# Adding the causal mask of the plain scores on VectorE instead of TensorE in an audio tower's three causal attentions

## The chip, the cores and the metric

The kernel runs on one core of one Trainium2 chip. The metric is the device time of one execution in microseconds (us); the time quoted for a kernel is the median of its runs.

## What is computed

A whole audio encoder: a tokenizer turns 32 utterances of 375 frames into 93 tokens of 256 features, and four layers follow, each an attention-like part and a feed-forward part. What matters here are the four softmax attentions. Three of them are causal, and the mask stands in the reference like this:

```
# layer 0 (16 heads of 16)
scores = jnp.einsum('bhqd,bhkd->bhqk', q, k) * scale
scores = jnp.where(causal[None, None], scores, -jnp.inf)
probs = jax.nn.softmax(scores / TEMP, axis=-1)
# layer 1 (16 heads of 16)
att = jnp.where(causal, att, jnp.float32(-jnp.inf))
att = jax.nn.softmax(att, axis=-1)
# layer 2 (32 maps of 8, taken from each other in pairs)
att = jnp.where(causal, att, -jnp.inf)
att = jax.nn.softmax(att, axis=-1)
```

The attention in the last feed-forward part (16 heads) has no mask. In the kernel's names they are `gattn` (layer 0, gated), `rattn` (layer 1), `dattn` (layer 2, differential) and `eattn` (the one without a mask).

## The kernel before

The layers run one after another on all 32 utterances, with barriers between them. All four attentions share one set of functions, one per engine, and one class `Attention` with their tiles and semaphores. An utterance has 93 tokens; its maps (16, or 32 in `dattn`) are worked on in units of 4, so that one PSUM bank holds 4 x 93 = 372 columns. A unit pair takes the two banks of `ps_s` (plain scores, query on the partitions) and later the two of `ps_t` (transposed scores, key on the partitions). An utterance has 2 pairs in `gattn`, `rattn` and `eattn`, and 4 in `dattn`.

The plain scores serve only for the row maximum. `maximum` (L677) on VectorE (DVE) reduces each bank to 4 negated maxima per row; `split` writes them as two bf16 parts, TensorE (PE) turns them (`turn_max`, L551), `max_t` (L692) copies them out, and the products with `sel` (L570) add them to the transposed scores. ScalarE (ACT) takes the exponential (L657), and the products of `weigh` (L584) make outputs and denominators: 17 columns wide, with a weight load of 93 columns each.

The mask of the plain scores is a product. Before the 8 score products of a pair, PE multiplies a bf16 identity by `mask_q` (0 or -1e30), 372 columns, into each bank (L536), and the scores (L542) add to it. The transposed scores get their mask in `gattn` and `rattn` through `sel` and `maxT` ("merged"), in `dattn` through products with `mask_k` (L559); this stays.

Each engine's order is written out by hand as a software pipeline. In its step for utterance b, PE makes the scores of utterance b+1 pair by pair and the transposed scores and weighted sums of b. Ahead of the last pair's transposed scores it turns the context of utterance b-1 (`turn_ctx`, L595), behind them comes the output projection of b-1 (`project`, L607), and `turn_max` of b+1 ends the step. DVE takes, for each pair, the two maxima of b+1 and then one piece of `behind`, the work on the context of b-1. In `gattn`, `rattn` and `eattn` that is one piece after the first pair: reciprocal and product (L919 and L920 in `gattn`). In `dattn` there are three: `context` after pair 0 (L1484 to L1488), `difference` after pair 1 (L1492 to L1495), then GpSimd (POOL) takes an inverse root (L1420), and `finish` after pair 2 makes the context (L1502). `turn_ctx` waits for it (`ctx_ready`). PE may write the next pair's scores when the maxima of the last pair are taken (`maxed`).

Of the kernel before, what the change touches and what calls it, by code (L numbers as in the profile page):

```python
# [24 lines left out]
ALU = mybir.AluOpType  # L25
AX = mybir.AxisListType

P = 128
# [3 lines left out]
T = 93  # L32
# [4 lines left out]
GT = GU * T  # L37
# [5 lines left out]
class Chain:  # L43


    def __init__(self, eng, sem, base=0):
        self.eng, self.sem, self.base = eng, sem, base
# [249 lines left out]
def measure_dve(dve, shared, b, added, count):  # L297

    dve.wait_ge(added, count)
    dve.bn_stats(shared["stat"][0:T, b, :], shared["hidden"][0:T, b, :])  # L300
# [48 lines left out]
class Attention:  # L349
# [11 lines left out]
    def __init__(self, s, maps, causal, exp_scale):  # L361
        self.maps, self.causal, self.exp_scale = maps, causal, exp_scale
        self.width = D // maps
        self.variants = P // 2 // self.width
        self.units = maps // 4
        self.banks_o = maps // HEADS
        self.q_all = s.sb("q_all", [P, DC, B * T])
        self.k_all = s.sb("k_all", [P, DC, B * T])
        self.v = s.sb("v", [P, B, HEADS, HD + 1])
        self.q = s.sb("q", [P, 2, DC, self.variants, T])  # L370
        self.k = s.sb("k", [P, 2, DC, T])
        self.only = s.sb("only", [P, self.variants])
        self.sel = s.sb("sel", [P, maps, T], BF16)
        self.negmax = s.sb("negmax", [P, maps])

        self.split_width = 2 * maps if maps == HEADS else 2 * maps + 2
        self.split = s.sb("split", [P, self.split_width], BF16)


        self.merged = causal and 2 * maps + T <= P  # L380
        self.maxT = s.sb("maxT", [P, T], BF16)
        self.probs = s.sb("probs", [P, 4, GT])
        self.rden = s.sb("rden", [P, self.banks_o, HEADS])
        self.ctx = s.sb("ctx", [P, 2, D])
        self.ctxT = s.sb("ctxT", [P, DC, T])
        if causal:
            self.mask_q = s.sb("mask_q", [P, 4, T], BF16)
            if not self.merged:
                self.mask_k = s.sb("mask_k", [P, 4, T], BF16)
        self.ps_s = s.ps("scores", [P, 2, 512])  # L390
        self.ps_t = s.ps("scoresT", [P, 2, 512])
        self.ps_o = s.ps("outputs", [P, 2, 512])
        self.ps_g = s.ps("general", [P, 2, 512])
        self.const_ready = s.sem("att_const")
        self.q_done = s.sem("q_done")
        self.k_done = s.sem("k_done")
        self.v_done = s.sem("v_done")
        self.q_ready = s.sem("q_ready")
        self.k_ready = s.sem("k_ready")
        self.v_ready = s.sem("v_ready")  # L400
        self.v_gated = None
        self.ranks_ready = None
        self.cut_ready = s.sem("cut_ready")
        self.scored = s.sem("scored")
        self.maxed = s.sem("maxed")
        self.split_ready = s.sem("split_ready")
        self.max_turned = s.sem("max_turned")
        self.maxT_ready = s.sem("maxT_ready")
        self.scoredT = s.sem("scoredT")
        self.probs_ready = s.sem("probs_ready")  # L410
        self.weighed = s.sem("weighed")
        self.outputs_read = s.sem("outputs_read")
        self.ctx_ready = s.sem("ctx_ready")
        self.ctx_turned = s.sem("ctx_turned")
        self.ctxT_ready = s.sem("ctxT_ready")
        self.out_done = s.sem("out_done")
        self.added = s.sem("added")
        self.biased = s.sem("biased")
        self.half_split = s.sem("half_split")
        self.step = s.sem("att_step")  # L420
# [13 lines left out]
def over_utterances(eng, body):  # L434


    body(0, 0, True, False)
    with eng.Fori(0, B // 2 - 1) as i:
        for j in range(2):
            body(2 * i + j + 1, 1 - j, False, False)  # L440
    body(B - 1, 1, False, True)
# [34 lines left out]
def attention_constants_dve(dve, a, ident):  # L476

    rows = ident[:, :].rearrange("p (h v e) -> p v h e", h=2, v=a.variants)
    dve.tensor_reduce(a.only[:, :], rows, AX.XY, ALU.add).then_inc(a.step, 1)
    dve.sem_inc(a.maxed, 2)  # L480
    dve.sem_inc(a.probs_ready, 2)
    dve.sem_inc(a.weighed, 4)
    dve.sem_inc(a.scoredT, 2 * a.units)
    dve.sem_inc(a.outputs_read, 3 - a.banks_o)
# [42 lines left out]
def attention_pe(pe, a, ident, ident16, w_out, before_out=None, extra_out=None):  # L527


    def scores(b, buf, p):  # L530
        if 2 * p % (a.units // DC) == 0:
            pe.wait_ge(a.cut_ready, DC * b + (2 * p * DC // a.units + 1))
        pe.wait_ge(a.maxed, b * a.units + (2 * p + 2))
        if a.causal:
            for half in range(2):
                pe.matmul(a.ps_s[0:T, half, 0:GT], ident16[:, 0:T], a.mask_q[:, :, :], start=True, stop=False,  # L536
                          skip_group_check=True)
        for j in range(4):
            for half in range(2):
                c, _, v = a.place(2 * p + half)  # L540
                rows = slice(half * P // 2, (half + 1) * P // 2)
                mm = pe.matmul(a.ps_s[0:T, half, j * T:(j + 1) * T], a.q[rows, buf, c, v + j, :], a.k[rows, buf, c, :],  # L542
                               start=not a.causal, stop=True, skip_group_check=True)
                if j == 3:
                    mm.then_inc(a.scored, 1)

# [85 lines left out]
    for p in range(a.units // 2):  # L632
        scores(0, 0, p)
# [36 lines left out]
def attention_dve(dve, a, steps, contexts, add, finish=None, shared=None):  # L670

    def maximum(b, w):
        dve.wait_ge(a.scored, b * a.units + (w + 1))
        dve.tensor_reduce(a.negmax[0:T, a.first_map(w):a.first_map(w) + 4],  # L677
                          a.ps_s[0:T, w % 2, 0:GT].rearrange("p (j t) -> p j t", j=4), AX.X, ALU.max,
                          negate=True).then_inc(a.maxed, 1)

    def split(b):
        dve.wait_ge(a.maxed, 2 + (b + 1) * a.units)
        dve.tensor_copy(a.split[0:T, 0:a.maps], a.negmax[0:T, :]).then_inc(a.half_split, 1)
        dve.wait_ge(a.half_split, b + 1)
        dve.tensor_tensor(a.split[0:T, a.maps:2 * a.maps], a.negmax[0:T, :], a.split[0:T, 0:a.maps],
                          ALU.subtract).then_inc(a.split_ready, 1)
        dve.wait_ge(a.split_ready, b + 1)

    def max_t(b):
        dve.wait_ge(a.max_turned, b + 1)  # L690
        dve.wait_ge(a.scoredT, a.units * (b + 2))
        dve.tensor_copy(a.maxT[0:2 * a.maps, :], a.ps_g[0:2 * a.maps, 0, :].bitcast(BF16)[:, 0:T]).then_inc(a.maxT_ready, 1)  # L692

    def behind(b, buf, p):

        if p == 0:
            dve.wait_ge(a.weighed, 4 + a.units * (b + 1))
            steps.begin(b)
        if p < len(contexts):
            contexts[p](b, buf)  # L700
        if p == len(contexts) - 1:
            steps.end()
        if p == len(contexts) and finish is not None:
            finish(b, buf)

    def utterance(b, buf, first, last):
        for p in range(a.units // 2):
            if not last:
                maximum(b + 1, 2 * p)
                maximum(b + 1, 2 * p + 1)  # L710
            if not first:
                behind(b - 1, 1 - buf, p)
        if not last:
            split(b + 1)
        if not first:
            add(b - 1)
        if not last:
            max_t(b + 1)
        if not first and shared is not None:
            measure_dve(dve, shared, b - 1, a.added, b)  # L720

    for w in range(a.units):
        maximum(0, w)
    split(0)
    max_t(0)
    over_utterances(dve, utterance)
    for p in range(a.units // 2):
        behind(B - 1, 1, p)
    add(B - 1)
    if shared is not None:  # L730
        measure_dve(dve, shared, B - 1, a.added, B)
# [66 lines left out]
def gated_attention(nc, shared, dram):  # L798
# [3 lines left out]
    with Scope(nc, "gattn") as s:  # L802
# [16 lines left out]
        with nc.Block() as block:  # L819
# [49 lines left out]
            @block.vector  # L869
            def _(dve):  # L870
                attention_constants_dve(dve, a, ident)
                norm_statistics_dve(dve, n, hidden, EPS)

# [315 lines left out]
def layer1_attention(nc, shared, dram):  # L1189
# [4 lines left out]
    with Scope(nc, "rattn") as s:  # L1194
# [18 lines left out]
        with nc.Block() as block:  # L1213
# [106 lines left out]
            @block.vector  # L1320
            def _(dve):
                attention_constants_dve(dve, a, ident)
                dve.memset(rows[0:TP, :, :, :], 0.0).then_inc(rows_clear, 1)
                norm_statistics_dve(dve, n, hidden, 1e-5, True)
# [1380 lines left out]
```

## Time and profile before

| | |
|---|---|
| median of 3 runs | 4446.45 us (4444.82 to 4450.03) |
| the profiled execution's own time | 4441.89 us |
| its span, first to last instruction | 4440.2 us |
| PE busy (matmul) | 3466.3 us, 78% |
| DVE busy | 2241.4 us, 50% |
| ACT busy | 1150.8 us, 26% |
| POOL busy | 1169.3 us, 26% |
| mean granted TensorE clock | 0.845 of 2.4 GHz |

How to read it: the rows of the views below count time from the span's start, and give an instruction (or a run of like ones, "x16") with its start, its length, its engine, its line in the kernel and "tile written <- tiles read". PE is TensorE's matmul, PEld its weight load. An f32 product shows as two matmul records, so the 8 score products of a pair are "x16". PEclk is the clock that TensorE was granted in a stretch, as a share of 2.4 GHz: 1.00 is that level, 0.50 is 1.2 GHz.

### The profile page before, as it was taken

Reading aid. Unit: us, or ns where it says so; the run is one execution under the profiler, and the core shown is the slowest. Engines: PE = TensorE matmul, PEld = TensorE weight load, DVE = VectorE, ACT = ScalarE, POOL = GpSimd, SP = SyncE. Lnnn points to the kernel's source line nnn. Section 1 sums busy time; section 2 is a strip of 40 time slices with the busy share of each in tenths; the row PEclk is TensorE's granted clock in tenths of the full one; section 3 lists DMA queues with packets and bytes.
Section 4 is the critical chain, followed back from the end, with each engine's and each line's share of the span. In section 5 each row is a group of like instructions: output and inputs, shape, how many; then the busy total and the mean of one; then the engine's idle time right before and its main releaser. Section 6 shows DMA issues by size and latency. Waiting matters only on the chain. (4 is left out here: it accounts for less than half of the span.)

```text
span 4440.2 us, 70612 instructions
## 1 busy us (share of the span) xinstructions
PE 3466.3 (78%) x23831; PEld 2262.3 (51%) x23832; DVE 2241.4 (50%) x4136; ACT 1150.8 (26%) x2267; POOL 1169.3 (26%) x904
## 2 busy tenths in 40 slices
PE   7589954669975999998149961678887788759999
PEld 3367732347753677776139951333333333245777
DVE  0444455224443355554523333478988889941343
ACT  2221110111211122122224420344433444303222
POOL 0112211011211233332530026344444444510121
PEclk9798866778888999998579985789888888869999
DMA  1000002630002000001521112000000000000000
GB/s 43 11 1 0 0 2 43 99 42 0 0 11 83 1 0 0 0 0 33 148 52 47 47 47 56 28 21 25 25 21 21 21 24 25 14 22 0 7 10 11
DMA packets 241137, 115.45 MB, mean 26 GB/s; under 512 B 174305, under 2 KB 225315, under 8 KB 241040
## 3 DMA queue, kind: packets, MB, share of 16 engines
q1 hardware_dynamic: 221136, 98.04, 8.9%
q0 software_dynamic: 18432, 12.40, 1.2%
q10 hardware_dynamic: 1472, 3.85, 0.3%
q8 instruction: 44, 0.72, 0.1%
q14 instruction: 53, 0.43, 0.0%
HBM read 79.03 MB, written 35.02 MB: 26 GB/s over the span
## 5 line engine op out<-in xcount | busy, mean ns | idle before, releaser
L2107 POOL TENSOR_TENSOR ssm_dBx<-ssm_du,ssm_b_wide 128x1488 f32<-128x1488 f32 x128 | 430.1, 3363 | 325.9 <-DVE ssm_state L2364 324.5
L2364 DVE TENSOR_TENSOR_SCAN ssm_state<-ssm_dA,ssm_dBx 128x372 f32<-128x372 f32 x512 | 434.2, 909 | 34.8 <-ACT ssm_dA L2175 19.5
L2254 PE MATMUL ssm_y<-ssm_hC,top_ident 128*128 128x512 f32 (+1 forms) x768 | 430.6, 706 | 9.0 <-DVE ssm_hC L2369 7.5
L2175 ACT ACTIVATE ssm_dA<-ssm_delta,ssm_decay 128x368 f32<-128x368 f32 x512 | 283.1, 568 | 575.0 <-DVE ssm_state L2364 559.5
L2254 PEld LDWEIGHTS ssm_y<-ssm_hC,top_ident 128*128 128x128 f32 x768 | 161.3, 225 | 253.2 <-issue 231.1
L2369 DVE TENSOR_TENSOR ssm_hC<-ssm_state,ssm_c_wide 128x1488 f32<-128x1488 f32 x128 | 218.1, 1704 | 71.4 <-issue 38.2
L657 ACT ACTIVATE dattn_probs<-dattn_scoresT 93x372 f32<-93x372 f32 x256 | 108.1, 472 | 415.4 <-PE dattn_scoresT L570 415.4
L2240 PE MATMUL ssm_c_wide<-ssm_dbc,ssm_pick 48*128 48x372 f32 x256 | 129.9, 592 | 107.0 <-DVE ssm_hC L2369 105.5
L677 DVE TENSOR_REDUCE dattn_negmax<-dattn_scores 93x4 f32<-93x372 f32 x256 | 127.1, 536 | 158.7 <-PE dattn_scores L542 158.7
L1830 POOL DMA_INDIRECT tiles_got<-moe_back,moe_slot x64 | 89.8, 1403 | 376.1 <-DMA moe_back<-tiles_y 356.9
L584 PE MATMUL dattn_outputs<-dattn_v,dattn_probs 93*93 (+1 forms) x2048 | 185.8, 233 | 0.0
L584 PEld LDWEIGHTS dattn_outputs<-dattn_v,dattn_probs 93*93 93x93 f32 x2048 | 181.9, 163 | 3.4
L1420 POOL TENSOR_TENSOR dattn_square<-dattn_square,top_minus_half 93x16 f32<-93x16 f32 x32 | 92.7, 2897 | 289.2 <-DVEq L1496 289.2
L501 POOL TENSOR_TENSOR rattn_q<-rattn_q_all,rattn_only 128x372 f32<-128x372 f32 x64 | 51.8, 809 | 439.5 <-PE rattn_scoresT L570 247.1
L2218 PE MATMUL ssm_misc<-ssm_xT,ssm_w_tap 128*128 128x364 f32 (+3 forms) x512 | 164.8, 475 | 2.6 <-ACT ssm_conv L2133 2.0
L501 POOL TENSOR_TENSOR eattn_q<-eattn_q_all,eattn_only 128x372 f32<-128x372 f32 x64 | 51.8, 809 | 406.9 <-PE eattn_scoresT L570 219.8
L501 POOL TENSOR_TENSOR dattn_q<-dattn_q_all,dattn_only 128x744 f32<-128x744 f32 x64 | 91.7, 1433 | 210.0 <-PE dattn_scoresT L570 115.5
L501 POOL TENSOR_TENSOR gattn_q<-gattn_q_all,gattn_only 128x372 f32<-128x372 f32 x64 | 51.8, 809 | 332.4 <-PE gattn_scoresT L570 247.9
L1546 PE MATMUL tiles_hidden<-tiles_x_part,moe_w 128*128 128x256 bf16 x496 | 136.3, 275 | 3.0 <-DVE tiles_x_part L1912 3.0
L1924 DVE TENSOR_TENSOR tiles_act<-tiles_gelu,tiles_act 128x512 bf16<-128x512 f32 x124 | 85.8, 692 | 102.1 <-ACT tiles_act L1850 102.1
L1547 PE MATMUL tiles_hidden<-tiles_x_part,moe_w 128*128 128x256 bf16 x496 | 136.3, 275 | 0.0
L1548 PE MATMUL tiles_hidden<-tiles_x_part,moe_w 128*128 128x256 bf16 x496 | 136.2, 275 | 0.0
(545 smaller groups left out, 7451.3 us busy)
## 6 DMA issues: line engine op xcount, KB each, us to landing
ssm_b_wide<-b_rows SPq DMA_DIRECT2D x64, 372.0 KB, 3.4
route_stage<-in_L_ffn_W SPq DMA_DIRECT2D x32, 512.0 KB, 4.3
qkv_rows<-rattn_rows SPq DMA_DIRECT2D x32, 288.0 KB, 3.0
rattn_heads<-qkv_rows SPq DMA_DIRECT2D x96, 96.0 KB, 3.4
moe_sent<-top_blank SPq DMA_DIRECT2D x1, 7936.0 KB, 23.7
tiles_x_in<-moe_sent SPq DMA_DIRECT2D x31, 256.0 KB, 2.8
moe_back<-tiles_y SPq DMA_DIRECT2D x31, 256.0 KB, 2.1
tok_frames<-in_frames ACTq DMA_DIRECT2D x8, 376.0 KB, 8.0
```

The lines of the kernel that those rows point to most:

```text
L501: pool.tensor_tensor(a.q[:, buf, c, :, :], a.q_all[:, c, bass.ds(b * T, T)].unsqueeze(1).broadcast_to([P, a.variants, T]), a.only[:, :].un ...
L584: mm = pe.matmul(a.ps_o[0:T, bank, h * (HD + 1):(h + 1) * (HD + 1)], a.probs[0:T, w % 4, j * T:(j + 1) * T], a.v[0:T, b, h, :], start=True ...
L1546: pe.matmul(out, w_high, x_high, start=start, stop=False)
L1547: pe.matmul(out, w_high, x_low, start=False, stop=False)
L1548: return pe.matmul(out, w_low, x_high, start=False, stop=stop)
L2107: pool.tensor_tensor(dBx[:, k % 2, :, :], du[:, :, :], b_wide[:, q % BUFS, k % 2, :].unsqueeze(1).broadcast_to([P, CC, GT]), ALU.mult).the ...
L2175: act.activation(by_utterance(dA[:, ring(k, c), 0:GT])[:, :, 1:], by_utterance(delta[:, c, :])[:, :, 1:], ACT.Exp, scale=decay[:, c, k:k + ...
L2218: mm = pe.matmul(by_utterance(ps_m[:, 0:GT])[:, :, back:], w_tap[:, TAPS - 1 - back, c, m * P:(m + 1) * P], by_utterance(n.xT[:, c, :])[:, ...
L2240: pe.matmul(ps_c[:, 0:GT], pick[:, k, :], dbc[:, j, :], start=True, stop=True).then_inc(c_ready, 1)
L2254: mm = pe.matmul(ps_y[:, at], ident[:, :], hC[:, k % 2, :, :].rearrange("p c t -> p (c t)")[:, at], start=(k == 0), stop=(k == N - 1))
L2364: dve.tensor_tensor_scan(state[:, k % 2, c, :], dA[:, ring(k, c), 0:GT], dBx[:, k % 2, c, :], 0.0, ALU.mult, ALU.add).then_inc(scanned, 1)
L2369: dve.tensor_tensor(hC[:, k % 2, :, :], state[:, k % 2, :, :], ps_c[:, 0:GT].unsqueeze(1).broadcast_to([P, CC, GT]), ALU.mult).then_inc(hc ...
```

## The change

DVE adds the mask. `scores` on PE loses the mask products, and its score products start the bank themselves. On DVE, `maximum` becomes `maxima`, which takes a pair at once: for each of the two banks an addition of the bank (PSUM) and `mask_q` (SBUF, bf16) into a new f32 tile `masked` in SBUF, then the two reductions, which now read `masked`. PE may write the next pair's scores when both additions are done (`scores_masked`), and no longer waits for the reductions. `eattn`, without a mask, only has its waits and reductions written pair by pair.

```
-        pe.wait_ge(a.maxed, b * a.units + (2 * p + 2))
-        if a.causal:
-            for half in range(2):
-                pe.matmul(a.ps_s[0:T, half, 0:GT], ident16[:, 0:T], a.mask_q[:, :, :], start=True, stop=False,
-                          skip_group_check=True)
+        pe.wait_ge(a.scores_masked if a.causal else a.maxed, b * a.units + (2 * p + 2))
...
-                               start=not a.causal, stop=True, skip_group_check=True)
+                               start=True, stop=True, skip_group_check=True)
...
-    def maximum(b, w):
-        dve.wait_ge(a.scored, b * a.units + (w + 1))
-        dve.tensor_reduce(a.negmax[0:T, a.first_map(w):a.first_map(w) + 4],
-                          a.ps_s[0:T, w % 2, 0:GT].rearrange("p (j t) -> p j t", j=4), AX.X, ALU.max,
-                          negate=True).then_inc(a.maxed, 1)
+    def maxima(b, p):
+        for w in (2 * p, 2 * p + 1):
+            dve.wait_ge(a.scored, b * a.units + (w + 1))
+            if a.causal:
+                dve.wait_ge(a.maxed, b * a.units + (w + 1))
+                dve.tensor_tensor(a.masked[0:T, w % 2, :, :], a.ps_s[0:T, w % 2, 0:GT].rearrange("p (j t) -> p j t", j=4),
+                                  a.mask_q[0:T, :, :], ALU.add).then_inc(a.scores_masked, 1)
+        for w in (2 * p, 2 * p + 1):
+            if a.causal:
+                dve.wait_ge(a.scores_masked, b * a.units + (w + 3))
+                found = a.masked[0:T, w % 2, :, :]
+            else:
+                found = a.ps_s[0:T, w % 2, 0:GT].rearrange("p (j t) -> p j t", j=4)
+            dve.tensor_reduce(a.negmax[0:T, a.first_map(w):a.first_map(w) + 4], found, AX.X, ALU.max,
+                              negate=True).then_inc(a.maxed, 1)
...
             if not last:
-                maximum(b + 1, 2 * p)
-                maximum(b + 1, 2 * p + 1)
+                maxima(b + 1, p)
```

On PE, one step of `gattn` ahead of `turn_ctx`, before:

```order
L536 MATMUL gattn_scores<-gattn_mask_q,top_ident 93x372 x2
L542 MATMUL gattn_scores<-gattn_k,gattn_q 93x93 x8
L564 MATMUL gattn_scoresT<-gattn_q,gattn_k 93x372 x2
L570 MATMUL gattn_scoresT<-gattn_maxT,gattn_sel 93x93 x8
L536 MATMUL gattn_scores<-gattn_mask_q,top_ident 93x372 x2
L542 MATMUL gattn_scores<-gattn_k,gattn_q 93x93 x8
L595 MATMUL gattn_general<-top_ident,gattn_ctx 128x93 x2
```

and of the change:

```order
L541 MATMUL gattn_scores<-gattn_k,gattn_q 93x93 x8
L563 MATMUL gattn_scoresT<-gattn_q,gattn_k 93x372 x2
L569 MATMUL gattn_scoresT<-gattn_maxT,gattn_sel 93x93 x8
L541 MATMUL gattn_scores<-gattn_k,gattn_q 93x93 x8
L594 MATMUL gattn_general<-top_ident,gattn_ctx 128x93 x2
```

Both pairs of mask products are gone, one of them between the first pair's scores and `turn_ctx`.

On DVE, the first pair of a step of `gattn` and the context that `turn_ctx` waits for, before:

```order
L677 TENSOR_REDUCE gattn_negmax<-gattn_scores 93x4
L676 REGISTER_ALU
L677 TENSOR_REDUCE gattn_negmax<-gattn_scores 93x4
L697 ISA
L919 RECIPROCAL gattn_rden<-gattn_outputs 93x16
L747 ISA
L920 TENSOR_TENSOR gattn_ctx<-gattn_outputs,gattn_rden 93x256
```

and of the change:

```order
L679 TENSOR_TENSOR gattn_masked<-gattn_scores,gattn_mask_q 93x372
L676 REGISTER_ALU
L679 TENSOR_TENSOR gattn_masked<-gattn_scores,gattn_mask_q 93x372
L683 REGISTER_ALU
L687 TENSOR_REDUCE gattn_negmax<-gattn_masked 93x4
L683 REGISTER_ALU
L687 TENSOR_REDUCE gattn_negmax<-gattn_masked 93x4
L706 ISA
L927 RECIPROCAL gattn_rden<-gattn_outputs 93x16
L755 ISA
L928 TENSOR_TENSOR gattn_ctx<-gattn_outputs,gattn_rden 93x256
```

Two additions stand between the scores and everything that DVE does after them.

On DVE in `dattn`, from the second pair of a step to the work ahead of POOL's inverse root, of the change (before, only two reductions from `dattn_scores` and the register instructions stood ahead of the `dattn_diff` rows):

```order
L679 TENSOR_TENSOR dattn_masked<-dattn_scores,dattn_mask_q 93x372 x2
L683 REGISTER_ALU
L687 TENSOR_REDUCE dattn_negmax<-dattn_masked 93x4
L683 REGISTER_ALU
L687 TENSOR_REDUCE dattn_negmax<-dattn_masked 93x4
L1500 TENSOR_TENSOR dattn_diff<-dattn_diff 93x256
L755 REGISTER_ALU
L1501 TENSOR_TENSOR dattn_diff<-dattn_diff 93x256
```

The additions of pairs 0 and 1 both stand ahead of that root.

## Rows read from the trace of the kernel before

**Rows 1.** Busy time by stretch, three loops: us, PE, PEld, DVE, ACT, POOL, PEclk, DMA share, GB/s

```profile
283.00:596.00 313.00, 307.00 (x3062) 222.44 (x3061) 131.55 (x365) 62.17 (x154) 60.86 (x120) 0.88 0.00 0
1490.00:2061.00 571.00, 569.66 (x6157) 404.57 (x6156) 289.58 (x700) 117.25 (x278) 189.93 (x150) 0.97 0.00 0
4136.00:4423.00 287.00, 280.94 (x3114) 220.44 (x3115) 120.67 (x336) 68.94 (x184) 60.87 (x120) 0.98 0.03 10
```

**Rows 2.** Tile views of the split maxima: turn_max, count, first and last start

```profile
L551 PE MATMUL gattn_general<-top_ident,gattn_split x32: 202/202/262, 282.2 to 595.9; 93*32 93x93 bf16 x32
L551 PE MATMUL dattn_general<-top_ident,dattn_split x32: 209/209/289, 1489.5 to 2061.4; 93*66 93x93 bf16 x32
```

**Rows 3.** Timeline of gattn, two utterances at clock 1.00: start us, us, engine, line

```profile
403.39 0.51 PE L536 MATMUL gattn_scores<-gattn_mask_q,top_ident 128*93 128x372 bf16 x2
404.76 0.99 DVE L677 TENSOR_REDUCE gattn_negmax<-gattn_scores 93x4 f32<-93x372 f32 x2 [0.68 <-PE gattn_scores L542]
405.67 0.24 DVE L919 RECIPROCAL gattn_rden<-gattn_outputs 93x16 f32<-93x16 f32 x1
405.81 0.52 PE L536 MATMUL gattn_scores<-gattn_mask_q,top_ident 128*93 128x372 bf16 x2
405.95 0.42 DVE L920 TENSOR_TENSOR gattn_ctx<-gattn_outputs,gattn_rden 93x256 f32<-93x256 f32 x1
406.25 0.90 PE L542 MATMUL gattn_scores<-gattn_k,gattn_q 64*93 64x93 f32 x16
407.08 0.38 PE L595 MATMUL gattn_general<-top_ident,gattn_ctx 93*128 93x93 f32 x2
...
421.86 0.85 PE L536 MATMUL gattn_scores<-gattn_mask_q,top_ident 128*93 128x372 bf16 x2
```

**Rows 4.** Timeline of eattn, context and its turn

```profile
4306.08 0.42 DVE L2628 TENSOR_TENSOR eattn_ctx<-eattn_outputs,eattn_rden 93x256 f32<-93x256 f32 x1
4306.76 0.38 PE L595 MATMUL eattn_general<-top_ident,eattn_ctx 93*128 93x93 f32 x2
```

**Rows 5.** Timeline of rattn, an utterance that begins at clock 0.50

```profile
1183.55 0.85 PE L536 MATMUL rattn_scores<-rattn_mask_q,top_ident 128*93 128x372 bf16 x2 [0.36 <-issue]
1184.33 1.56 PE L542 MATMUL rattn_scores<-rattn_k,rattn_q 64*93 64x93 f32 x16
1187.12 0.42 DVE L1359 TENSOR_TENSOR rattn_ctx<-rattn_outputs,rattn_rden 93x256 f32<-93x256 f32 x1
1189.87 0.38 PE L595 MATMUL rattn_general<-top_ident,rattn_ctx 93*128 93x93 f32 x2
```

**Rows 6.** Timeline of dattn, one utterance at clock 1.00

```profile
1702.17 0.38 PE L595 MATMUL dattn_general<-top_ident,dattn_ctx 93*128 93x93 f32 x2
1707.94 0.90 PE L542 MATMUL dattn_scores<-dattn_k,dattn_q 64*93 64x93 f32 x16
1710.78 0.41 DVE L1488 TENSOR_TENSOR dattn_diff<-dattn_outputs,dattn_rden 93x256 f32<-93x256 f32 x1
1711.74 0.99 DVE L677 TENSOR_REDUCE dattn_negmax<-dattn_scores 93x4 f32<-93x372 f32 x2 [0.55 <-PE dattn_scores L542]
1714.32 2.90 POOL L1420 TENSOR_TENSOR dattn_square<-dattn_square,top_minus_half 93x16 f32<-93x16 f32 x1 [8.35 <-DVEq L1496]
1717.24 1.64 DVE L1502 TENSOR_TENSOR dattn_ctx<-dattn_diff,dattn_square 93x256 f32<-93x256 f32 x1 [0.32 <-POOL dattn_square L1420]
1720.03 0.38 PE L595 MATMUL dattn_general<-top_ident,dattn_ctx 93*128 93x93 f32 x2
```

**Rows 7.** Busy time by stretch, gattn: around a fall of the clock, and later falls

```profile
418.00:421.60 3.60, 3.60 (x40) 3.33 (x37) 0.85 (x3) 0.84 (x2) 1.02 (x2) 1.00 0.00 0
421.80:425.00 3.20, 3.20 (x23) 1.88 (x22) 1.33 (x4) 0.00 (x0) 0.00 (x0) 0.50 0.00 0
430.00:440.00 10.00, 9.63 (x75) 6.35 (x73) 3.94 (x10) 1.17 (x3) 1.01 (x2) 0.66 0.00 0
470.00:480.00 10.00, 9.63 (x80) 6.92 (x80) 2.99 (x8) 1.14 (x3) 1.82 (x4) 0.66 0.00 0
```

More of the change, by code:

```diff
@@ L387, in __init__ @@
             self.mask_q = s.sb("mask_q", [P, 4, T], BF16)
+            self.masked = s.sb("masked", [P, 2, 4, T])
             if not self.merged:
@@ L405, in __init__ @@
         self.maxed = s.sem("maxed")
+        self.scores_masked = s.sem("scores_masked")
         self.split_ready = s.sem("split_ready")
@@ L480, in attention_constants_dve @@
     dve.sem_inc(a.maxed, 2)
+    dve.sem_inc(a.scores_masked, 2)
     dve.sem_inc(a.probs_ready, 2)
@@ L720, in utterance @@
             measure_dve(dve, shared, b - 1, a.added, b)
-    for w in range(a.units):
-        maximum(0, w)
+    for p in range(a.units // 2):
+        maxima(0, p)
     split(0)
```

## The prediction

> **What bounds the kernel now.** The view of busy time by stretch comes first. In the loops of `gattn` and `dattn` TensorE is busy for 307.00 of 313 us and 569.66 of 571, VectorE for 42% and 51% [rows 1]: the order of TensorE sets the pace, and VectorE matters where TensorE waits for it. The same rows show the second thing: the granted clock was 0.88 in `gattn`, 0.97 in `dattn` and 0.98 in `eattn`. Then come the timelines, of which the reader is to see one thing above all: how long the context lies finished before TensorE turns it (`turn_ctx`). That is the margin which the change spends.
>
> **Removed: the mask products.** A pair of them holds TensorE from 405.81 to 406.25, 0.44 us [rows 3], and at half clock from 1183.55 to 1184.33, 0.78 us [rows 5]. There are 2 pairs per utterance in `gattn` and `rattn`, 4 in `dattn`, so 64 + 64 + 128 = 256 pairs, and 256 x 0.44 = 113 us if nothing were late. `eattn` keeps its instructions; I cost it at nothing.
>
> **Added: 512 additions on VectorE.** No row has an addition of 93 x 372 from PSUM. Two reductions of that size start at 404.76 and let the reciprocal start at 405.67: 0.455 us each from start to start; whole, they last 0.99/2 = 0.50 [rows 3]. An addition of 256 columns from PSUM and SBUF (L920) lasts 0.42 with its latency [rows 3]. I take 0.47 a piece, 0.94 a pair, with 0.91 and 1.0 as ends: nearest to the reduction's step, which streams as many columns from the same bank. The reductions now read SBUF; no row has that at this size, so I leave them at 0.91 a pair, and a gain of some 0.1 is inside the range. VectorE has room: 2 x 0.94 in a 9.2 us step that is 42% used, 4 x 0.94 in 18 that is 51% used. It does not become the bound by its sum, only by being late.
>
> **`gattn` and `rattn`, clock 1.00.** The context ends at 405.95 + 0.42 = 406.37, and TensorE turns it at 407.08: a margin of 0.71 [rows 3]. In the new order both additions stand ahead of the context (0.94 later), and TensorE arrives 0.44 earlier, since the second pair's mask products are gone; the first pair's moves both sides alike. From the context's end to the turn takes at most 4306.76 - 4306.50 = 0.26, as `eattn` shows, where TensorE came without waiting [rows 4]; I take 0.2, with 0.1 and 0.26 as ends. TensorE so waits 0.94 + 0.44 - 0.71 + 0.2 = 0.87 us, and has saved 2 x 0.44 = 0.88. Net 0.01 of a 9.235 us utterance ((421.86 - 403.39)/2) [rows 3]; between 0 and 0.1, that is 0 to 6 us over 64 utterances. What is queued behind the waiting instruction is all of the transposed scores, weighing and projection, so nothing hides it.
>
> **The same at half clock.** There the context ends at 1187.54 and the turn starts at 1189.87: margin 2.33 [rows 5]. The change spends 0.94 + 0.78 + 0.2 = 1.92. No wait, and both pairs are saved in full: 1.56 us. The clock falls again and again (0.66 in the ten us from 430 and again in those from 470 [rows 7], some 40 us apart), about one such utterance in four: 16 in the two loops, 16 x 1.56 = 25 us, if the falls stay as they are.
>
> **`dattn`, clock 1.00.** Count from the first pair's scores, 1707.94. VectorE ends `context` at 1711.19 (3.25) and idles 0.55 until the second pair's scores are there at 1711.74 (3.80) [rows 6]. Now the first additions push 3.25 to 4.19; the second scores are ready before that (3.80 - 0.44), so the next additions follow at once, and the reductions start at 5.13 instead of 3.80: 1.33 later. The third pair's 1.85 us of VectorE fit under the inverse root's 2.90 on POOL, which starts 1.33 later as well. The context, done at 1717.24 + 1.64 = 1718.88 (10.94) before, is done at 12.27. TensorE reaches the turn at 12.09 - 3 x 0.44 = 10.77. It waits 1.50 + 0.15 = 1.65 and has saved 4 x 0.44 = 1.76: 0.11 an utterance, 4 us over 32 (ends: 0 and 10).
>
> **The clock.** So at equal clock almost nothing is won, and what remains is what the new waits do to the clock. The fall at 421.8 came after 3.60 us in which TensorE was never idle and the clock stood at 1.00 [rows 7]; what ran there was weighing (17 columns wide), projection, weighing. `gattn` has that stretch every 9.2 us and a clock of 0.88; `dattn` has it every 18 and 0.97; `eattn` has two more wide products in it and 0.98 [rows 1]. The change gives every utterance a second weak stretch: in `dattn` weighing, one group of scores, then 1.65 us of nothing. I expect `dattn` to fall at least as often per us as `gattn` does now, and put it two points under `gattn`'s clock because TensorE stands idle in the new stretch: 0.86. The price is in two rows: `gattn` takes (595.9 - 282.2)/31 = 10.12 an utterance [rows 2] against 9.235 at full clock, so 12 points of clock cost 8.7%, 0.73% a point; `dattn`'s loop lasts (2061.4 - 1489.5)/31 x 32 = 590 us, 4.3 us a point, and 11 points are 47 us. In `gattn` and `rattn` the wait adds a weak stretch too, but a slow utterance no longer waits; of the 25 us I leave them 20, with -10 and 25 as ends.
>
> By the Trainium skill, "TensorE: Matmul & The Clock Gate", section "HAM oscillation — how this bites in real kernels", it is long idle gaps that bring the clock down; waits of 0.87 and 1.65 us would not. The trace disagrees as far as the fall at 421.8 goes, which had no gap before it. By that rule the sum would be the first rival's.
>
> **The sum.** -20 (`gattn`, `rattn`) - 4 (`dattn` at equal clock) + 47 (its clock) = +23 us. The profiled execution took 4441.89, its span 4440.2, so it would be 4465; it stood 4.6 below the median of 4446.45, so I forecast 4470. Its own range: from 4456 (a clock of 0.89 in `dattn`: 8 x 4.3 - 24 = +10) to 4500 (0.83 there and next to nothing saved in `gattn` and `rattn`: 14 x 4.3 - 4 = +56).
>
> **Rivals.**
> *The waits leave the clock alone.* For it: the new wait is short, and wide products stand on its far side. Against it: a fall without any gap, and a clock that is lower the closer the weak stretches lie [rows 1, 7]. Then the gains stand: -25 - 4 = -29, 4417. It decides at `dattn`'s clock: 29 us are eaten at 7 points, so at 0.90 or above the kernel is not slower. Chance 0.20.
> *It comes out even.* The clock gives back just what the masks gave: `dattn` near 0.91, 4446, within 9 us. 0.2% is what a measurement of this kernel can tell from no change. Chance 0.16.
> A third, that the additions hide altogether and 113 us go, would need the context to be in time; the margin of 0.71 against 1.58 speaks against it, and its chance, 0.02, is counted with the first.
>
> **The numbers.** Slower 0.64 (the forecast), same 0.16, faster 0.20. Cases of both signs hold the chance, so the range reaches from 4425, which takes in the even case and part of the first rival, to 4500; I leave some 0.13 out below and 0.07 above.
>
> **What would show it.** Right: 512 additions on VectorE near 0.55 us whole and 0.47 apart; TensorE waiting for the context's product ahead of `turn_ctx` once an utterance, some 0.9 us in `gattn` and 1.6 in `dattn`, at clock 1.00; an utterance of `dattn` at full clock still near 17.8 (17.86 between the turns at 1702.17 and 1720.03 [rows 6]); a clock in `dattn`'s loop below 0.90, its loop some 40 us longer, `gattn`'s and `rattn`'s each some 10 shorter. Wrong: a `dattn` loop at 0.95 or more, waits that are not there, or other layers' times moved.

## The result and the profile after

The changed kernel takes 4496.22 us (median of 5 runs, 4477.55 to 4514.65) against 4446.45 (5 runs, 4439.88 to 4450.03): 1.0116 times as long, 95% interval 1.0095 to 1.0137, or 50 us more. The forecast was 4470, 23 more, with a range from 4425 to 4500. So the sign came as forecast and the time lies inside the range, but the change was twice as large as forecast. The profiled execution took the median itself, 4496.22 us, with a span of 4494.5 and a mean clock of 0.826 (before: 4441.89, 4440.2 and 0.845).

The three loops of [rows 1] after the change, busy time by stretch (us, then PE, PEld, DVE, ACT, POOL, PEclk, DMA share, GB/s):

```profile
288.00:599.00 311.00, 293.71 (x2942) 226.05 (x2944) 198.93 (x495) 62.19 (x154) 60.82 (x120) 0.85 0.00 0
1484.00:2106.00 622.00, 600.93 (x5920) 442.43 (x5922) 399.03 (x953) 117.24 (x278) 189.86 (x150) 0.85 0.00 0
4183.00:4471.00 288.00, 279.95 (x3120) 219.16 (x3120) 121.11 (x338) 68.92 (x184) 60.78 (x120) 0.99 0.03 10
```

The tile views of `turn_max`, against [rows 2]:

```profile
L550 PE MATMUL gattn_general<-top_ident,gattn_split x32: 202/202/262, 288.5 to 598.4; 93*32 93x93 bf16 x32
L550 PE MATMUL dattn_general<-top_ident,dattn_split x32: 209/209/287, 1484.8 to 2105.3; 93*66 93x93 bf16 x32
```

VectorE's busy time rises from 290 to 399 us in `dattn`'s loop, by the 128 pairs of additions; TensorE's clock there falls from 0.97 to 0.85. Last less first start, `gattn`'s loop goes from 313.7 to 309.9 us, `dattn`'s from 571.9 to 620.5; `rattn`'s goes from 316.0 to 302.1 and `eattn`'s from 287.5 to 287.8. Together that is +31 us. The rest of the profile's 54 lies outside the loops, and most of it in one place. The waits by releaser between `gattn`'s and `rattn`'s loop (engine, line, tile, what it waited for: us, times, longest), before:

```profile
PEld rattn_scoresT L1282 <- DMA rattn_heads<-qkv_rows: 82.1, 8, 15.3
```

and after:

```profile
PEld rattn_scoresT L1290 <- DMA rattn_heads<-qkv_rows: 96.8, 8, 17.6
```

TensorE waits 14.7 us longer for the gather that lays out `rattn`'s heads, ahead of its loop, which the diff doesn't touch. The DMA issues of the same stretch (KB each, median us from issue to landing), before:

```profile
rattn_heads<-qkv_rows SPq DMA_DIRECT2D x96, 96.0 KB, 3.4
```

and after:

```profile
rattn_heads<-qkv_rows SPq DMA_DIRECT2D x96, 96.0 KB, 4.9
```

Smaller shares, in this execution alone: `eattn` from its last `turn_max` to the end of the span 23.6 instead of 16.6 us, at a clock of 0.62 after the change and of 0.97 before; the tokenizer 5 us.

Now the path that the prediction worked out. The timeline of `gattn` after the change, one utterance at clock 1.00, against [rows 3]:

```profile
400.78 0.99 DVE L679 TENSOR_TENSOR gattn_masked<-gattn_scores,gattn_mask_q 93x372 f32<-93x372 f32 x2 [0.62 <-PE gattn_scores L541]
401.69 0.97 DVE L687 TENSOR_REDUCE gattn_negmax<-gattn_masked 93x4 f32<-93x372 f32 x2
402.59 0.24 DVE L927 RECIPROCAL gattn_rden<-gattn_outputs 93x16 f32<-93x16 f32 x1
402.87 0.42 DVE L928 TENSOR_TENSOR gattn_ctx<-gattn_outputs,gattn_rden 93x256 f32<-93x256 f32 x1
403.40 0.38 PE L594 MATMUL gattn_general<-top_ident,gattn_ctx 93*128 93x93 f32 x2 [0.67 <-DVEq L931]
```

Two additions take 0.91 us from start to start (400.78 to 401.69), and TensorE, which came to the turn without waiting before, idles 0.67 us. In `dattn` (against [rows 6]):

```profile
1818.98 0.21 PE L550 MATMUL dattn_general<-top_ident,dattn_split 93*66 93x93 bf16 x1
1819.27 0.90 PE L541 MATMUL dattn_scores<-dattn_k,dattn_q 64*93 64x93 f32 x16
...
1826.79 2.90 POOL L1428 TENSOR_TENSOR dattn_square<-dattn_square,top_minus_half 93x16 f32<-93x16 f32 x1 [9.30 <-DVEq L1504]
...
1829.60 0.90 PE L541 MATMUL dattn_scores<-dattn_k,dattn_q 64*93 64x93 f32 x16
1829.72 1.65 DVE L1510 TENSOR_TENSOR dattn_ctx<-dattn_diff,dattn_square 93x256 f32<-93x256 f32 x1 [0.95 <-POOL dattn_square L1428]
1831.42 0.57 PE L594 MATMUL dattn_general<-top_ident,dattn_ctx 93*128 93x93 f32 x2 [0.92 <-DVE dattn_ctx L1510]
```

The root starts 7.52 us behind the first scores (1826.79 less 1819.27) where it started 6.38 behind them before; the last pair's scores are done, and TensorE idles 0.92 us for the context. The turn's own length tells what follows: 0.57 instead of 0.38. Busy time by stretch around that moment:

```profile
1817.60:1831.10 13.50, 12.82 (x157) 9.52 (x155) 10.53 (x25) 2.53 (x6) 4.32 (x3) 1.00 0.00 0
1831.20:1844.80 13.60, 13.38 (x75) 9.81 (x75) 4.91 (x14) 1.26 (x3) 1.93 (x3) 0.50 0.00 0
1844.90:1858.00 13.10, 12.74 (x151) 9.47 (x150) 10.37 (x25) 3.79 (x9) 5.88 (x4) 1.00 0.00 0
```

The clock falls right behind the wait and stands at 0.50 for 13.6 us, in which TensorE starts 75 matmuls instead of about 150. From about 1660 us on every second utterance goes this way: 18.5 and 22.45 us in turn, from `turn_max` to `turn_max`. In all, TensorE waits ahead of the turn in `dattn`'s loop (engine, line, what it waited for: us, times, longest):

```profile
PE dattn_general L594 <- DVE dattn_ctx L1510: 18.8, 29, 0.9
```

The waits of 0.9 alternate with waits of 0.35 in the utterances that began at half clock.

### The profile page after: what moved, and what is told of

Same layout as the page of the kernel before. It is cut to its first block and busy times, and to the rows that moved or that the text cites. A ratio compares the mean times of both kernels' runs of the same rounds, so it can differ in the third digit from the quotient of the medians.

```text
span 4494.5 us, 70811 instructions
## 1 busy us (share of the span) xinstructions
PE 3455.2 (77%) x23319; PEld 2295.5 (51%) x23320; DVE 2494.0 (55%) x4648; ACT 1150.8 (26%) x2267; POOL 1175.1 (26%) x904
## 5 line engine op out<-in xcount | busy, mean ns | idle before, releaser
L583 PEld LDWEIGHTS dattn_outputs<-dattn_v,dattn_probs 93*93 93x93 f32 x2048 | 212.3, 185 | 5.7
L583 PE MATMUL dattn_outputs<-dattn_v,dattn_probs 93*93 (+1 forms) x2048 | 214.5, 249 | 0.0
L679 DVE TENSOR_TENSOR dattn_masked<-dattn_scores,dattn_mask_q 93x372 f32<-93x372 f32 x256 | 126.7, 534 | 43.4 <-PE dattn_scores L541 42.3
```

What stands on the lines that cost most here:

```text
L583: mm = pe.matmul(a.ps_o[0:T, bank, h * (HD + 1):(h + 1) * (HD + 1)], a.probs[0:T, w % 4, j * T:(j + 1) * T], a.v[0:T, b, h, :], start=True ...
```

## The experiments

The theory: VectorE's additions make the context late, TensorE waits for it ahead of `turn_ctx`, and in `dattn` these waits bring the clock down; the gather's 15 us come from something else that the change brought. The rivals: VectorE's load itself; the missing wide products alone, with or without a wait; a cost that lies in no one place. Each experiment gives the whole time beside the kernel before on the same chip, and the loops from its own trace.

**One half at a time.** The additions in `dattn` alone, as below, and in `gattn` and `rattn` alone (there `by_dve = a.causal and a.merged`); where `by_dve` is false, TensorE's mask products and the reductions from PSUM are as before, but that the reductions wait for both banks of a pair:

```
     def maxima(b, p):
+        by_dve = a.causal and not a.merged
...
-            if a.causal:
+            if by_dve:
```

> The change in dattn alone; gattn and rattn keep TensorE's mask products. Theory (the late context makes TensorE wait ahead of turn_ctx in dattn and that lowers its clock): dattn's loop lasts 610 to 635 us as in the changed kernel (620.5), the loops of gattn and rattn 314 and 316 as before, the whole some 40 to 55 us over the kernel before. Rival (a third or more of the 50 us comes from what the change does outside the attention loops, by moving where the clock falls there): the loops read the same, but the whole stands under +35, or over +60.

> The change in gattn and rattn alone; dattn keeps TensorE's mask products. Theory: both loops win what they won in the changed kernel (313.7 to 309.9 and 316.0 to 302.1), dattn's stays at 572, and the whole is 10 to 25 us faster than the kernel before: this half of the change was a gain. Rival (the additions cost as much here, and the loops' gain is eaten by the places around them): within 9 us of the kernel before.

`dattn` alone: 4500.61 us, 1.0114 times before (1.0086 to 1.0143), its loop 604.1 us at clock 0.87 (below the 610 that was the least expected), the loops of `gattn` and `rattn` 314.4 and 315.5. `gattn` and `rattn` alone: 4462.99, 1.0032 (1.0022 to 1.0042), their loops 312.9 and 302.0, `dattn`'s 575.7. So the loss sits in `dattn`, as the theory has it, and the other half does win in its loops, 15 us; but the whole of that half was slower than before, which neither theory nor rival had. Both kernels show the slow gather (TensorE waits 96 and 97 us for it), the first one too, whose `rattn` is as before. That counted (below), the second kernel should stand near +2; its median stands 16 above before. In its profile `dattn`'s loop is 4 us longer and its end ran at half clock, 34 us instead of 23.5 from the last `turn_max` to the last instruction, which would fill the gap. But the kernel before with an unused tile (next) shows 576.0 there too, with no instruction changed, so 4 us is no more than the spread of that loop; where the 16 us come from stays open.

**The gather.** The new tile takes 2 x 4 x 93 x 4 = 2976 bytes of each partition, 46.5 times 64. All tiles reserved behind it move by that, and `heads`, into which the gather writes pieces of 16 elements, 64 bytes, came to lie 32 bytes off a multiple of 64. So the changed kernel with 32 bytes left free, and the kernel before with the tile reserved and never used:

```
             self.masked = s.sb("masked", [P, 2, 4, T])
+            s.sb("pad", [P, 8])
```

> The changed kernel, with 32 bytes per partition left free behind the new tile, so that every tile behind it starts on a multiple of 64 bytes again, as before the change (the new tile takes 2976 bytes, 46.5 x 64, and the heads of rattn's gather, written in pieces of 64 bytes, came to lie 32 bytes off). Theory (that offset is what makes rattn's gather slower): its median time to landing returns from 4.9 to 3.4 us, TensorE's wait for it from 96.8 to some 82 us, and the whole is 10 to 20 us faster than the changed kernel, near 4481; the attention loops stay as they are (620 in dattn). Rival (the gather is slower for another reason, such as its start against other transfers): 4.9 us and 4496 as before.

> The kernel before, with the new tile reserved in the three causal attentions and never used: no instruction is changed. Theory (the 32 bytes): the gather's landing goes from 3.4 to 4.9 us, TensorE's wait for it from 82 to 96 us, all four attention loops as before, and the whole is 11 to 17 us slower than the kernel before. Rival: no difference, within 9 us.

The DMA issues of the first of these:

```profile
rattn_heads<-qkv_rows SPq DMA_DIRECT2D x96, 96.0 KB, 3.4
```

and of the second:

```profile
rattn_heads<-qkv_rows SPq DMA_DIRECT2D x96, 96.0 KB, 4.9
```

Reserving the tile alone costs what was expected: 4463.78 us, 1.0033 times before (1.0021 to 1.0046), with no instruction changed, and TensorE waits 96.4 us for the gather. Mending it brings the landing back to 3.4 us and the wait to 84.8. The whole of the mended kernel, 4487.79 (1.0079, 1.0055 to 1.0103), is 8 us under the changed one's, where 10 to 20 were expected; the two kernels spread by 35 us each over their runs (their `dattn` loops alone were 628 and 620 us), so the total by itself would not have decided it. The rows and the unused tile do.

**TensorE's wait, taken away in two ways.** First by useless work: `dattn` keeps its mask products, which the scores write over. Then by no mask at all on `dattn`'s plain scores:

```
         pe.wait_ge(a.scores_masked if a.causal else a.maxed, b * a.units + (2 * p + 2))
+        if a.causal and not a.merged:
+            for half in range(2):
+                pe.matmul(a.ps_s[0:T, half, 0:GT], ident16[:, 0:T], a.mask_q[:, :, :], start=True, stop=True,
+                          skip_group_check=True)
```

> The changed kernel, but in dattn TensorE still makes the two mask products of each pair, whose result the score products then write over: 56 us of TensorE's work that nothing needs, VectorE as in the changed kernel. Theory (wait and clock): TensorE reaches turn_ctx 1.3 us later, the wait there falls from 1.65 us to some 0.3, the clock in dattn returns to 0.94 or more, and dattn's loop falls from 620 to 575 to 595 us, so the kernel with more work is 25 to 45 us faster than the changed one. Rival (the additions themselves, VectorE's load beside POOL and ScalarE, cost the time): dattn's loop stays at 620 or grows, and the whole is no faster than the changed kernel.

> In dattn nothing masks the plain scores: no product, no addition, so the row maxima are taken over all keys there (the transposed scores keep their mask); gattn and rattn as in the changed kernel. Theory (it is the wait that brings the clock down): no wait ahead of turn_ctx, a full-clock utterance of dattn near 16.1 us (17.86 less 4 x 0.44), a clock of 0.94 or more, the loop 500 to 535 us. Rival (it is the missing wide products that bring the clock down, with or without a wait): no wait either and 16.1 at full clock, but a clock of 0.88 or less and a loop of 545 to 575 us.

`dattn`'s loop with the useless products:

```profile
1497.00:2079.00 582.00, 580.89 (x6160) 409.94 (x6158) 422.30 (x948) 117.25 (x278) 190.35 (x150) 0.95 0.00 0
```

and without a mask:

```profile
1496.00:2025.00 529.00, 527.55 (x5910) 392.05 (x5910) 289.48 (x700) 117.15 (x278) 189.80 (x150) 0.97 0.00 0
```

With 56 us of work added the kernel is 30 us faster than the changed one, 4466.27 against 4496.22 (1.0037 times before, 1.0019 to 1.0056); no wait ahead of the turn is left, where 0.3 us was expected, and VectorE works no less (422 us), so its load is not the cost. The loop does not come all the way back to the 571.9 of the kernel before: with no wait at all, utterances of 17.91 and 19.64 us alternate from end to end, as they do in part of the loop before (17.86 and 19.65). Without a mask the wide products are just as much gone as in the changed kernel, and the clock is 0.97: in `dattn` their absence alone does not bring it down either. The whole took 4413.83 us (0.9920, 0.9907 to 0.9932).

**The wait, put back by measure.** The next kernels start from the one below (reductions behind the context, no wait in `dattn`, clock 0.97). In `dattn` VectorE makes one or three additions more ahead of the difference, whose sums nothing reads; the third kernel gives TensorE six wide products in the time that it would wait:

```
+                if not a.merged and w == 3:
+                    for i in range(3):
+                        dve.tensor_tensor(a.dummy[0:T, i, :, :],
+                                          a.ps_s[0:T, w % 2, 0:GT].rearrange("p (j t) -> p j t", j=4),
+                                          a.mask_q[0:T, :, :], ALU.add)
```

> e6_reductions_last with one addition more on VectorE in dattn, of a pair's second bank into a place that nothing reads, ahead of the difference of the context: 0.46 us of delay on the way to turn_ctx, TensorE's own work unchanged (in e6_reductions_last the turn came 0.05 us after the context, with no wait to speak of). Theory (waits there lower the clock): a wait of some 0.45 us per utterance, 14 us in the loop by itself, and the clock of dattn falls from 0.973 to 0.92 to 0.96: loop 550 to 570 us instead of 530. Rival (a wait costs itself and no more): clock 0.96 or more, loop 540 to 548.

> The same with three such additions, 1.4 us of delay, about the wait of the changed kernel. Theory: 43 us of waiting in the loop by itself, and a clock of 0.84 to 0.90: loop 600 to 640 us, the whole 70 to 110 us over e6_reductions_last. Rival (a wait costs itself and no more): clock 0.96 or more, loop 565 to 582, the whole 35 to 50 us over.

> e10_delay3 with six wide products on TensorE ahead of the last pair's scores in dattn, which those scores write over: 1.3 us of work that nothing needs, in the time in which TensorE waited. The context is as late as in e10_delay3. Theory (it is TensorE's idleness there, not the late context, that lowers the clock): clock 0.94 or more and a loop of 570 to 590 us, 30 us or more below e10_delay3. Rival (the late context lowers it in another way, or the clock does not matter): as long as e10_delay3 or longer.

`dattn`'s loop with one addition more, by stretch:

```profile
1461.00:2032.00 571.00, 562.45 (x5918) 415.53 (x5918) 431.49 (x980) 117.16 (x278) 189.82 (x150) 0.91 0.00 0
```

and TensorE's waits ahead of the turn in it (us, times, longest):

```profile
PE dattn_general L598 <- DVE dattn_ctx L1528: 7.5, 16, 0.5
```

The loop with three:

```profile
1442.00:2071.00 629.00, 606.09 (x5914) 433.35 (x5914) 447.39 (x1041) 117.16 (x278) 189.82 (x150) 0.84 0.00 0
```

and its waits:

```profile
PE dattn_general L598 <- DVE dattn_ctx L1528: 22.6, 29, 0.8
```

The loop with three and the wide products:

```profile
1456.00:2038.00 582.00, 572.86 (x6096) 419.24 (x6096) 464.22 (x1041) 117.24 (x278) 189.82 (x150) 0.95 0.00 0
```

and its waits:

```profile
PE dattn_general L603 <- DVE dattn_ctx L1533: 8.0, 20, 0.4
```

For `dattn` this settles that such waits bring the clock down. Waits of at most 0.5 us, 7.5 us in all, make the loop 41 us longer (529.9 to 570.7, a little over the expected 570, at a clock under the expected 0.92); waits of at most 0.8, 22.6 in all, make it 99 longer. The waits themselves came to half of what was expected, 14 and 43 us. With the wide products the loop is 53 longer, of which up to 40 is that work (31 x 1.3) and 8.0 are waits that remain. These are as much waiting as with one addition more, and yet the clock is 0.95 and not 0.91: wide work ahead of a wait counts, and not the sum of the waits alone. How much of it is the filled time and how much the wide products, these runs don't part. The whole: 4414.10, 4464.03 and 4410.15 us, against 4450.66 for the kernel before beside them. The loop grows by 4.4 to 5.4 times what TensorE waited, and most of that is the clock.

**A version that is faster than both.** Only the additions have to stand ahead of the context; the reductions have time until `split`:

```
             if not last:
-                maxima(b + 1, p)
+                masks(b + 1, p)
+                if not a.causal:
+                    maxima(b + 1, p)
             if not first:
                 behind(b - 1, 1 - buf, p)
+            if not last and a.causal:
+                maxima(b + 1, p)
```

> The changed kernel with the 32 bytes mended, eattn's reductions written as before, and on VectorE the two reductions of a pair moved behind the piece of the context that follows the pair, so that only the two additions stand ahead of it. Theory (the context's delay is the cost): in gattn and rattn the context is no later than before (additions in the place of the reductions), TensorE does not wait ahead of turn_ctx, and a full-clock utterance takes 8.4 us instead of 8.88; in dattn the context is 0.4 us later than before the change instead of 1.33, the wait falls from 1.65 to 0.7, a full-clock utterance takes 16.8 to 17.0, the clock is 0.90 or more and the loop 545 to 580 us. The whole 4385 to 4430. Rival (VectorE's load and the missing wide products set the time, whatever the order): dattn's loop at 600 or more, gattn's and rattn's above 300, the whole 4450 or more.

> As e6_reductions_last, and in dattn the masked scores have four places instead of two, so that the reductions of the first two pairs go behind the difference, under POOL's inverse root. Theory: the additions alone cost the context of dattn nothing against the kernel before, TensorE comes 1.32 us earlier to a margin of 1.0, waits 0.3, a full-clock utterance takes 16.4 to 16.6, the clock is 0.93 or more, and the loop lasts 515 to 550 us; the whole 4355 to 4405. Rival (VectorE is now the bound, or PE waits for the additions ahead of the next pair's scores): 17.2 us or more per full-clock utterance and no better than e6_reductions_last.

The first takes 4355.00 us, 0.9790 times before (0.9774 to 0.9806): 95 us faster than the kernel before and 141 than the changed one, better than the theory's range of 4385 to 4430, and `dattn`'s loop of 529.9 better than its 545 to 580. Its three causal loops:

```profile
280.00:574.00 294.00, 287.54 (x2940) 222.01 (x2940) 193.98 (x493) 62.13 (x154) 60.71 (x120) 0.85 0.00 0
932.00:1228.00 296.00, 290.18 (x2938) 223.86 (x2939) 192.52 (x491) 62.15 (x154) 60.71 (x120) 0.84 0.00 0
1447.00:1976.00 529.00, 527.37 (x5908) 391.35 (x5908) 422.09 (x948) 117.15 (x278) 189.79 (x150) 0.97 0.00 0
```

and the end of an utterance of `dattn` in its timeline:

```profile
1714.03 1.64 DVE L1520 TENSOR_TENSOR dattn_ctx<-dattn_diff,dattn_square 93x256 f32<-93x256 f32 x1 [0.95 <-POOL dattn_square L1438]
...
1714.81 0.90 PE L542 MATMUL dattn_scores<-dattn_k,dattn_q 64*93 64x93 f32 x16
...
1715.72 0.38 PE L595 MATMUL dattn_general<-top_ident,dattn_ctx 93*128 93x93 f32 x2
```

The context is done at 1715.67, the turn starts at 1715.72, behind the scores and with no idle time of TensorE shown: the wait of 0.7 that I expected was not there, and so the clock stayed whole. VectorE does the same additions and reductions as in the changed kernel; their order (and some 3 us in `eattn`) made the 4488 of the mended kernel into 4355. `gattn` and `rattn`, without waits too, stand at a clock of 0.85 and 0.84 where they had 0.88 and 0.87 before: there the missing wide products do cost some clock by themselves. And there the waits of the changed kernel left no mark on the clock that these runs show. It waited in `gattn` and in `rattn`

```profile
PE gattn_general L594 <- DVEq L931: 12.1, 18, 0.7
PE rattn_general L594 <- DVEq L1370: 11.4, 17, 0.7
```

and stood at 0.85 and 0.87 with these waits, at 0.85 and 0.84 without them. That waits lower the clock is shown in `dattn` alone. The second version, with the reductions of two pairs behind the difference, has no wait to take away any more and gains nothing: 4363.23 us, 0.9809 (0.9791 to 0.9826).

## Why the prediction came out as it did

**The additions: right.** Forecast 0.47 from start to start and near 0.55 whole; measured 0.455 and 0.53 (a row of the page, the 256 of `dattn`):

```profile
L679 DVE TENSOR_TENSOR dattn_masked<-dattn_scores,dattn_mask_q 93x372 f32<-93x372 f32 x256 | 126.7, 534 | 43.4 <-PE dattn_scores L541 42.3
```

**`gattn` and `rattn`: right in kind.** The wait was 0.67 instead of 0.87, so a full-clock utterance gained 0.16 (9.04 to 8.88) instead of 0.01, but `gattn`'s clock fell from 0.88 to 0.85, which the 20 us did not hold. The loops won 17.7 us in the profiled execution, and between 3 and 16 in the four other kernels that have the same two loops; so the term of -20 was some 7 too good on the mean.

**`dattn` at equal clock: right net, by two errors that cancel.** I took a saving of 1.76 and a wait of 1.65. The kernel without a mask shows a full-clock utterance of 16.61 against 17.86, so the four pairs are worth 1.25, not 1.76 (1.37 in every second utterance, 18.13 to 16.76). The turns of the kernel without a mask:

```profile
1695.59 0.38 PE L594 MATMUL dattn_general<-top_ident,dattn_ctx 93*128 93x93 f32 x2
1712.20 0.38 PE L594 MATMUL dattn_general<-top_ident,dattn_ctx 93*128 93x93 f32 x2
```

Part of the pairs' time went into other handovers, as behind `turn_max`, where the mask products followed after 0.04 us before the change and the scores now follow after 0.29 (1818.98 to 1819.27):

```profile
1707.48 0.21 PE L551 MATMUL dattn_general<-top_ident,dattn_split 93*66 93x93 bf16 x1
1707.52 0.49 PE L536 MATMUL dattn_scores<-dattn_mask_q,top_ident 128*93 128x372 bf16 x2
```

TensorE so came to the turn 11.23 behind the first scores, not 10.77, and the context was done at 12.10, not 12.27: the wait was 0.92, not 1.65. The net was 0.2 to 0.27 (utterances of 17.65 and 17.59) instead of 0.11.

**`dattn`'s clock: right in kind, its size by luck.** 0.86 forecast, 0.85 measured, and the loop 48.6 longer against -4 + 47 = 43; over the three kernels with this loop as changed, +32 to +56, on the mean 46. The reason given, idleness in a weak stretch, is what the waits put in by measure show; the weak stretch alone, with no wait, does nothing in `dattn`. But 0.86 was taken from `gattn`'s clock and from a wait of 1.65 in every utterance, 53 us in the loop, and the loop had 18.8. Since more waiting went with a lower clock (0.91 with 7.5 us in the loop, 0.84 with 22.6), a right clock from nearly three times the waiting is luck. By the Trainium skill, "TensorE: Matmul & The Clock Gate", section "HAM oscillation — how this bites in real kernels", it takes long gaps; here no wait ahead of the turn in `dattn`'s loop was over 0.92 us. The same page's section "A second HAM failure mode: psum-queue depth-cycling" tells of another kernel whose frequent short idling makes the clock swing, and the runs of `dattn` agree with that one: 0.97 without waits, 0.91 with waits of at most 0.5 us.

**The sum: the step that failed.** Its terms gave +23 and measured +31 in the loops, but its list was short. The place of the new tile was costed nowhere, and is 14 us (the unused tile: 4463.78 against 4449.77). "`eattn` keeps its instructions; I cost it at nothing" missed 0.1 us per utterance: its reductions now go behind both banks' waits, and a full-clock utterance takes 9.14 instead of 9.03. In the kernels written that way the loop took 287.8 to 292.2 us, in those that kept the old order 284.7 to 287.7, some 3 us. With means: -13 + 46 + 14 + 3 = +50, as measured, where the forecast had -20 - 4 + 47. That it meets the 50 to the microsecond is chance: `dattn`'s loop alone ran from 604 to 628 us in the three kernels, and each mean is taken against one profile of the kernel before. "Other layers' times moved" stood in the prediction as a sign against it, and they did move.

**The rivals.** That the waits leave the clock alone is refuted: `dattn` stood at 0.85, not at 0.90 or more. That it comes out even needed 0.91. That the additions hide altogether needed another order on VectorE, and with that order most of the 113 us did go: 95.

## What to carry to other kernels

Work that is moved to an engine with room costs by what it is put ahead of, not by its length: follow the chain to the engine that sets the pace, and put on that chain only what must be there. A short idle gap on TensorE, in a stretch where it already has little wide work, can cost several times its length through the clock, as in `dattn`, so even waits of half a microsecond are worth a look; in `gattn` and `rattn` waits of 0.7 cost no clock, so look at the clock of each loop with and without them. Reserving a tile moves every tile behind it; look whether the destinations of DMAs in small pieces keep their alignment.

## What the runs showed of the hardware that I had not expected

A gather into SBUF in pieces of 64 bytes landed in a median of 3.4 us where its tile began on a multiple of 64 bytes, and in 4.9 where it began 32 off; TensorE's wait for it went from 82 or 85 to 96 or 97 us. The two places that were aligned and the one that was not were all that I tried.

The price of a wait was the other: 7.5 us of waits in pieces of at most 0.5 took the clock of `dattn` from 0.97 to 0.91 and cost 41 us. With wide products ahead of the waits, 8.0 us of them left it at 0.95.
